# A graph network on one core: VectorE's early operations reordered and thinned, filler matmuls on TensorE, later epilogues

## The reference

```python
msg = concat([x[dst], x[src], edge_attr]) @ W + b      # per edge
h   = relu(segment_sum(msg, dst))                      # per node
```

## Time and profile before

| | us |
|---|---|
| median of 3 runs | 204.44 (204.09 to 204.75) |
| the profiled execution's own time | 204.8 |
| its span, first to last instruction | 202.9 |
| TensorE matmul busy | 172.5 (85%) |
| VectorE busy | 170.4 (84%) |
| ScalarE busy | 119.3 (59%) |
| GpSimd busy | 34.0 (17%) |
| chain of waits, by engine | PE 61%, DVE 31%, issue 3%, DMA 2%, ACT 2% |

### The profile page before, as it was taken

The page is one execution under the profiler, slowest core; times in us unless marked ns, Lnnn a source line. Parts: engine busy times, 40 slices in busy tenths (PEclk is TensorE's granted clock), DMA queues, the critical chain, the costliest instruction groups (busy, mean ns, idle before and its releaser), DMA issues.

```text
span 202.9 us, 5018 instructions
## 1 busy us (share of the span) xinstructions
PE 172.5 (85%) x2019; PEld 163.2 (80%) x2019; DVE 170.4 (84%) x420; ACT 119.3 (59%) x234; POOL 34.0 (17%) x58
## 2 busy tenths in 40 slices
PE   0414389799999999999999999999996999999950
PEld 0103379788999999989899999899996999999940
DVE  0898999999999999999999979921039999999874
ACT  2236657678899999998898999984310201121101
POOL 8478832000400240006006000000000000000000
PEclk9999999999999999999999999999999999999995
DMA  1334210000000000000000000000000010011010
GB/s 42 105 84 126 59 14 3 0 3 3 3 0 4 0 0 3 3 2 3 0 1 3 3 0 3 2 3 0 3 0 0 5 38 3 7 36 25 22 24 19
DMA packets 8959, 3.34 MB, mean 16 GB/s; under 512 B 8168, under 2 KB 8485, under 8 KB 8935
## 3 DMA queue, kind: packets, MB, share of 16 engines
q1 hardware_dynamic: 8135, 2.07, 4.9%
q0 software_dynamic: 800, 0.93, 1.8%
HBM read 2.18 MB, written 0.81 MB: 15 GB/s over the span
## 4 chain that ended last, share of the span: by engine, by line
PE 61%; DVE 31%; issue 3%; DMA 2%; ACT 2%; DVEq 0%; ACTq 0%
PE acc L989 17%; PE pset L1035 17%; DVE oh L517 15%; PE pset L975 12%; PE acc L1035 7%; PE epb L1018 2%; PE epb L1029 2%; DMA adj<-in_dst 2%; DVE adj L508 2%; PE epb L1006 2%; DVE adj L470 1%; DVE u L546 1%; DVE x L531 1%; ACT u L843 1%; DVE adj L456 1%
## 5 line engine op out<-in xcount | busy, mean ns | idle before, releaser
L517 DVE TENSOR_TENSOR oh<-iota,keys 128x2000 bf16<-128x2000 bf16 (+1 forms) x79 | 90.9, 1179 | 1.0 <-ACT keys L811 0.5
L828 ACT ACTIVATE adj<-pset 125x1000 bf16<-125x1000 f32 (+7 forms) x100 | 81.4, 840 | 13.8 <-PE pset L975 11.9
L989 PE MATMUL acc<-x,adj 125*125 125x195 bf16 x625 | 67.9, 252 | 0.0
L975 PE MATMUL pset<-oh 128*125 128x125 bf16 x625 | 53.8, 230 | 9.0 <-DVE oh L517 8.9
L989 PEld LDWEIGHTS acc<-x,adj 125*125 125x125 bf16 x625 | 57.3, 139 | 0.3
L975 PEld LDWEIGHTS pset<-oh 128*125 128x125 bf16 x625 | 47.8, 146 | 11.9 <-ACT adj L828 4.9
L1035 PE MATMUL pset<-z,adj 125*125 125x192 bf16 x425 | 36.8, 246 | 1.8 <-DVE x L673 1.8
L1035 PEld LDWEIGHTS pset<-z,adj 125*125 125x125 bf16 x425 | 35.5, 136 | 2.0 <-DVE x L673 2.0
L917 ACT ACTIVATE x<-x 125x192 f32<-125x192 f32 (+2 forms) x6 | 2.6, 428 | 34.5 <-DVE x L682 34.5
L1035 PE MATMUL acc<-z,adj 125*125 125x192 bf16 x200 | 17.5, 246 | 0.0
L1035 PEld LDWEIGHTS acc<-z,adj 125*125 125x125 bf16 x200 | 16.8, 136 | 0.0
(11 more groups left out here) (123 smaller groups left out, 159.9 us busy)
## 6 DMA issues: line engine op xcount, KB each, us to landing
x_nat<-in_x_tiles SPq DMA_DIRECT2D x1, 406.2 KB
x_nat<-in_x_tiles SPq DMA_DIRECT2D x1, 375.0 KB
out<-x SPq DMA_DIRECT2D x2, 187.5 KB
out<-x SPq DMA_DIRECT2D x3, 93.8 KB
adj<-in_dst SPq DMA_DIRECT2D x1, 208.5 KB
out<-x SPq DMA_DIRECT2D x1, 125.0 KB
adj<-in_edges,adj POOLq DMA_INDIRECT x5, 4.6
adj<-in_edge_attr,adj POOLq DMA_INDIRECT x5, 3.4
```

The source lines that it names most:

```text
L517: dve.tensor_tensor(out=oh[k % 3][:, 0:n, :, :], in0=iota2[:, 0:Q, :].unsqueeze(1).broadcast_to([128, n, Q, 2]), in1=keys[:, k * SET:k * S ...
L828: ins = act.activation(adj4[0:Q, g, :, i * WD:(i + n) * WD].rearrange("p h (w e) -> p h w e", e=WD), rows[:, w - k * SET:w - k * SET + n, ...
L975: ins = pe.matmul(pset[k % 2][0:Q, i // 4, i % 4 * 128:i % 4 * 128 + WD * G], oh[k % 3][:, i, :, 0], oh[k % 3][:, i, :, 1], start=True, st ...
L989: ins = pe.matmul(acc[g % 2][0:Q, 0:XW], adj4[0:Q, g, h, :], x3[:, h, :], start=(h == 0), stop=(h == G - 1))
```

## The change

- L446 goes from VectorE to ACT, and `offset` uses an operation with one input in place of two; `ones` is gone. Part 4's offset is put behind the first keys.
- `rest_of_x`, `low_of_x` and `bias_rest` of the first part stand ahead of the first one-hot; `rest_of_x(1)`, `low_of_x(1)` and `bias_rest(1)` stand behind sets 3, 5 and 7.
- The distances of parts 1 to 4 are ACT's (`distances`, five blocks ahead of the key block).
- The mask operations on VectorE are gone; SP issues nine small SBUF-to-SBUF DMAs that lay the bias rows in `bw`, once ACT has cast the third part.
- `KEY_BLOCK` and `SUM_SET` are later; part 0's attribute sums go one by one behind sets 10 to 14. Epilogues 0 and 1 turn at blocks 18 and 25 (13 and 22 before); the others keep their block. ACT does `scale_x` one block earlier.
- Layer 1 begins when the first part of x is split; it waits for the second at group 12. In block 0, set 4 is built behind layer 1's matmuls.
- TensorE gets filler matmuls of 512 columns on a zeroed piece of `adj`: 10 at the very start, 9 between the picks and the first key transposes, 4 behind these, 1 behind each of the sets 1 to 3.
- `base_of` for groups 0 to 15 stands ahead of the last two `z_rest`/`z_low`; the rest behind batch 0. The last step of a batch is two operations over all its groups in place of one per group.

```diff
-KEY_BLOCK = {1: 5, 2: 20, 3: 38, 4: 48}
-SUM_SET = {1: 12, 2: 25, 3: 41, 4: 51}
+KEY_BLOCK = {1: 7, 2: 22, 3: 38, 4: 48}
+SUM_SET = {0: 10, 1: 17, 2: 29, 3: 45, 4: 54}
+TURN = (18, 25, 32, 41, 50, 60, 69, 78, 82)
...
+        still = adj[:, 4 * G * Q:4 * G * Q + 512]
...
+            dve.memset(still, 0.0).then_inc(still_ready, 1)
             dve.wait_ge(dst_in, 16)
-            dve.tensor_scalar(rows16[:, 0:EC], dst_rows[:, 2:EC + 2], -float(MID), None, ALU.add).then_inc(rowsf_ready, 1)
...
-                link(dve.scalar_tensor_tensor(out=junk[:, j, :], in0=row[:, 0:EC], scalar=thr_mid[:, j:j + 1],
-                                              in1=ones[:, :], op0=ALU.is_lt, op1=ALU.mult,
-                                              accum_out=cnt2[:, j:j + 1]))
+                link(dve.tensor_scalar(junk[:, j, :], row[:, 0:EC], thr_mid[:, j:j + 1], None, ALU.is_lt, ALU.add,
+                                       accum_out=cnt2[:, j:j + 1]))
...
-            for j in range(1, J):
+            for j in range(1, 4):
                 offset(j)
...
+            rest_of_x(0, 0, XA)
             key_distances(0)
             key_tiles(0)
             key_sums(0)
-            rest_of_x(0, 0, XA)
+            low_of_x(0, 0, XA)
+            offset(4)
+            bias_rest(0)
             dve.wait_ge(consts, 7)
             dve.wait_ge(keys_ready, 1)
             onehots(0)
             onehots(1)
-            bias_rest(0)
-            low_of_x(0, 0, XA)
             onehots(2)
+            onehots(3)
             rest_of_x(1, XA, G)
-            bias_rest(1)
-            attr_sums(0, 0, WD)
-            onehots(3)
-            low_of_x(1, XA, G)
-
-            for k in range(4, NSETS):
+            onehots(4)
+
+            for k in range(5, NSETS):
...
-                if k == 10:
...
+                if k == 5:
+                    low_of_x(1, XA, G)
+                if k == 7:
+                    bias_rest(1)
                 for j in range(1, J):
                     if k == KEY_BLOCK[j] + 2:
-                        key_distances(j)
+                        dve.wait_ge(dist_ready, j)
+                        key_tiles(j)
                     if k == KEY_BLOCK[j] + 3:
-                        key_tiles(j)
-                    if k == KEY_BLOCK[j] + 4:
                         key_sums(j)
...
+            base_of(0, BATCHES[1][1])
+            base_of(BATCHES[1][1], BATCHES[2][1])
             z_rest(last - 1)
...
-                for k in range(n):
-                    ins = dve.tensor_scalar(f_v[i % 2][:, k, :], f_p[:, k, 0:C], f_c[:, k:k + 1], f_r[:, k:k + 1],
-                                            ALU.subtract, ALU.mult)
-                flink(ins)
+                flink(dve.tensor_tensor(o, p, c.unsqueeze(2).broadcast_to([Q, n, C]), ALU.subtract))
...
+                flink(dve.tensor_tensor(vv, o, r.unsqueeze(2).broadcast_to([Q, n, C]), ALU.mult))
...
+            act.wait_ge(dst_in, 16)
+            act.activation(rows16[:, 0:EC], dst_rows[:, 2:EC + 2], ACT.Copy, bias=-float(MID)).then_inc(rowsf_ready, 1)
...
-            for j in range(1, J):
-                copy_row(j)
+            copy_row(1)
+            copy_row(2)
             cast_x(0, 0, XA)
+            for j in range(3, J):
+                copy_row(j)
+            cast_bias(0)
+            cast_middle_x(0, 0, XA)
             copy_keys(acc[0][:, 0:2 * Q], 0)
-            cast_middle_x(0, 0, XA)
+            cast_bias(1)
+            def distances(j):
+                act.wait_ge(pairs_in[j], 16)
+                act.activation(d_f[:, j, :], pairs[:, j, 1::2], ACT.Identity, bias=thr_neg[:, j:j + 1])
+                act.activation(q_f[:, j, :], pairs[:, j, 0::2], ACT.Copy, scale=1.0 / Q, bias=-float(Q // 2) / Q)\
+                   .then_inc(dist_ready, 1)
...
+                if w <= 6 * G < end:
+                    act.wait_ge(bw_in, 16 * 3 * EP)
...
-                    if b == turn_block(i) - 1:
+                    if b == turn_block(i) - 2:
                         scale_x(i)
...
+            def keep_going(n):
+                for _ in range(n):
+                    pe.matmul(epb[:, 1, :], still[:, 0:128], still, start=True, stop=True)
+            keep_going(10)
...
+            keep_going(9)
             turn_keys(acc[0], 0)
+            keep_going(4)
...
                     if g == 0:
-                        pe.wait_ge(xl_ready, 2)
+                        pe.wait_ge(xm_ready, 1)
+                        pe.wait_ge(xl_ready, 1)
...
+            sp.wait_ge(bp_ready, 3)
+            for m in range(EP):
+                for part in range(3):
+                    mine = slice(VFROM + m * KB + part, VFROM + (m + 1) * KB, 3)
+                    sp.dma_start(bw[mine, m, :], bpart[mine, part, :]).then_inc(bw_in, 16)
```

More of the change, by code:

```diff
@@ L627, in _ @@
             z_low(last - 2)
-            reduce_sums(G - 1)
-            z_rest(last - 1)
-            z_low(last - 1)
-            z_rest(last)
-            z_low(last)
-            dve.tensor_reduce(deg_sum[:, :], stats[:, :, 0], AX.X, ALU.add).then_inc(deg_ready, 1)
             fc = [0]
@@ L662, in _ @@
                 dve.wait_ge(se_in[j], 16)
-            dve.wait_ge(rest_ready, len(EPILOGUES))
             base_of(0, BATCHES[1][1])
+            base_of(BATCHES[1][1], BATCHES[2][1])
+            z_rest(last - 1)
+            z_low(last - 1)
+            z_rest(last)
+            z_low(last)
+            dve.tensor_reduce(deg_sum[:, :], stats[:, :, 0], AX.X, ALU.add).then_inc(deg_ready, 1)
             na = 0
@@ L716, in _ @@
                 if i == 0:
-                    base_of(BATCHES[1][1], G)
+                    base_of(BATCHES[2][1], G)
                 if i == 1:
@@ L793, in copy_row, with cast_bias @@
                 act.activation(row16[:, j, :], row[:, 0:EC + 1], ACT.Copy).then_inc(rows_copied, 1)
-            for j in range(1, J):
-                copy_row(j)
+            copy_row(1)
+            copy_row(2)
+            def cast_bias(k):
+                if k == 0:
+                    act.wait_ge(b_in, 16 * 2 * EP)
+                else:
+                    act.wait_ge(br_ready, k)
+                act.activation(bpart[VHALF:128, k, :], brows[VHALF:128, :] if k == 0 else brest[VHALF:128, k - 1, :], ACT.Copy).then_inc(bp_ready, 1)
             def cast_x(i, a, b):
@@ L868, in cast_middle @@
                 act.activation(z3[:, a:b, C:2 * C], u[i % 2][:, 0:b - a, 0:C], ACT.Copy).then_inc(mid_ready, 1)
-            def cast_bias(k):
-                if k == 0:
-                    act.wait_ge(b_in, 16 * 2 * EP)
-                else:
-                    act.wait_ge(br_ready, k)
-                act.activation(bpart[VHALF:128, k, :], brows[VHALF:128, :] if k == 0 else brest[VHALF:128, k - 1, :], ACT.Copy).then_inc(bp_ready, 1)
-            cast_bias(0)
             evacuate(0)
-            cast_bias(1)
             cast_x(1, XA, G)
-            evacuate(1)
-            cast_bias(2)
+            for k in range(1, LEAD):
+                evacuate(k)
             cast_middle_x(1, XA, G)
-            for k in range(2, LEAD):
-                evacuate(k)
             for b in range(NSETS):
@@ L888, in _ @@
                     evacuate(b + LEAD)
+                if b == 3:
+                    cast_bias(2)
+                for j in range(1, J):
+                    if b == KEY_BLOCK[j] - 5:
+                        distances(j)
                 for j in range(1, J):
@@ L988, in layer1 @@
                 for h in range(h0, h1):
+                    if g == 0 and h == XA:
+                        pe.wait_ge(xm_ready, 2)
+                        pe.wait_ge(xl_ready, 2)
                     ins = pe.matmul(acc[g % 2][0:Q, 0:XW], adj4[0:Q, g, h, :], x3[:, h, :],
@@ L1050, in _ @@
                     i += n
+                if b == 0:
+                    build(LEAD)
                 for j in range(1, J):
```

54 lines of the change are left out of this document (21 added, 33 removed).

## The result

The changed kernel takes 198.86 us (median of 6 runs, 198.11 to 199.45); the kernel before, run beside it, 204.41 (204.09 to 204.92). The ratio is 0.9724, with a 95% interval of 0.970 to 0.9748. Run again later it took 198.55, ratio 0.9713 (0.9697 to 0.973). The forecast was 198.6, with a range of 196.2 to 201.8. The profiled execution took 199.06, its span is 197.2.

What follows compares the result with a forecast made beforehand. VectorE was taken to bound building up to 46 us, TensorE afterwards. Gains of 3.7 (to layer 1's end), 2.0 and 0.1 sum to 5.8 off 204.8, giving 199.0, or 198.6 for the median; range 196.2 to 201.8.

Steps and rivals of the forecast that it cites:

- The start: Up to the first one-hot: gains and costs nearly cancel, one-hot 0 at 15.9 (15.99 before), bounds 15.0 and 16.8.
- VectorE's work up to set 16: First one-hot to set 16: 5.0 us leaves VectorE, 0.3 lost to waits; set 16 at 40.9, gain 4.8.
- Sets 17 to 21, the give-back: Sets 17 to 21: attribute sums load VectorE and epilogue 0 is still to be paid; 1.4 us lost, bounds 0.8 and 1.8.
- Set 22 to the end of layer 1: TensorE bounds here, only its gaps may go: 0.3 us gained, bounds 1.8 gained and 1.0 lost.
- The change to layer 2: After layer 1: base_of for 16 groups fills VectorE's idle 5.57, TensorE's 2.00 wait goes; gain 2.0, bounds 1.7 and 2.0.
- The last batch: Last batch: L711's three operations become two of 0.36; gain 0.1, bounds -0.1 and 0.3.
- The nine bias DMAs: On SP: nine issues of 0.3 us and a landing of some 3 end at 34; price nothing, cover 8 us.
- The offset's new form: VectorE's offsets: no change taken; by the skill each of four SBUF offsets might lose about 0.22 us, up to 0.7 lower.
- this rival: ACT becomes the bound: 0.5 to 1 us in each of three places; with ACT or a late start, 201.5, chance 0.20.
- The other sign: Building up to set 16: the forecast is wrong if set 16 comes later than 42.5.
- the key transposes that I had named: Set 27's key transposes, part 2 in block 22: no idle of TensorE expected, with a cover of 0.3 us.
- eight layer-1 matmuls in 0.69 in the first block: Layer 1's first block: a sign of the forecast, eight matmuls already taking 0.69 us, the higher clock level.

Runs made afterwards that it cites:

- run three: The changed kernel with ACT's copies of picked rows 3 and 4 ahead of its cast of x: 198.03 us, ratio 0.9702.
- run four: The changed kernel with the distances of parts 1 to 4 on VectorE again in place of ACT: 199.70 us, ratio 0.9764.
- five: The changed kernel with the bias rows laid by VectorE's masks behind set 10 again, without the nine DMAs: 201.54 us, ratio 0.9858.
- nine: The changed kernel with copied rows first, early turns, scale_x one block ahead, and part 0's attribute-sum round trip ahead of the bias DMAs: 196.55 us, ratio 0.9626.
- run ten: The changed kernel with copied rows first, early turns and part 0's attribute-sum round trip ahead of the bias DMAs, scale_x two blocks ahead: 195.84 us, ratio 0.9588.
- run seven: The changed kernel with ACT's scale_x one block ahead of the turn in place of two: 199.34 us, ratio 0.9742.
- six: The changed kernel with epilogues 0 and 1 at blocks 13 and 22, second key block at 20, part 0's sums behind sets 4 to 8: 198.38 us, ratio 0.9696.
- eight: The changed kernel with rows 3 and 4 copied before the x cast, early turns, key block and sums, and scale_x one block ahead: 198.15 us, ratio 0.9685.
- run two: The changed kernel without any of the 26 filler matmuls: 198.99 us, ratio 0.9733.

## Why the prediction was right, step by step

- **The start.** The pick chain is 0.94 earlier, as forecast (1.0), and ACT's 0.56 is near the 0.53 of the row it was taken from. The first fillers ended at 5.65 and the first pick stands at 5.80 with and without them, so they cost nothing. The open point was when x lands; it landed at 10.09, near the late end, and with the copies of rows 3 and 4 behind the cast the gain was gone. I put one-hot 0 at 15.9, inside bounds of 15.0 and 16.8, and it came at 16.61. This term was off by 0.7, and run three gave 0.7 to 0.8 back by moving one line. What was wrong is the weight: "if at 10 or 11 there is no gain" was in the text, and the value taken was nearer to the other end.
- **VectorE's work up to set 16.** Forecast 5.0 off and 0.3 lost, measured 4.62. Runs four and five put two terms back singly: the distances cost 0.46 (0.45), the masks 2.3 in all (2.16). The bound that the windows named is shown.
- **Sets 17 to 21, the give-back.** This term failed in size. Forecast was a loss of 1.4, with bounds of 0.8 and 1.8. The stretch took 6.72, and with epilogue 0's 2.0 still to be paid that is 0.6 more than the 8.12 before: outside the bounds. VectorE needed 6.7 us for the five sets in place of 7.5; one group sum fell into them and not two, and TensorE waited 0.23 once.
- **Set 22 to the end of layer 1.** Forecast 0.3 gained, measured 0.1 (2.69 - 0.80 = 1.89 lost, of which epilogue 0's 2.0 are not this term's). The sum hides two larger parts. Up to set 35 some 0.7 was lost, in the crowd where epilogues 0 and 1 and the key block stand close together; with the other 0.6 that is the 1.3 which runs nine and ten win back by moving the turns (together with the second key block and part 0's sums). From 35 on 0.80 was gained, where I had said that TensorE's own work is the bound. Run four gives 0.76 of it to the distances, 0.48 at one place; `scale_x` has only 0.14 there by run seven, its other 0.39 lie between 16 and 35.
- **The change to layer 2.** 1.97 of 2.0, and 1.8 to 2.0 in time by itself. The cover of `z_rest` held with 0.20 us left.
- **The last batch.** 0.11 for 0.1. The subtraction over three groups runs in the gap behind the first small operation:

```profile
193.22 0.16 DVE L687 TENSOR_TENSOR x<-x 125x3 f32<-125x3 f32 x1
193.30 0.35 DVE L689 TENSOR_TENSOR x<-x 125x192 f32<-125x192 f32 x1
...
194.07 0.36 DVE L694 TENSOR_TENSOR x<-x 125x192 f32<-125x192 f32 x1
```

- **The nine bias DMAs.** Forecast nine issues of 0.3 us and a cover of 8. They took 5.65, 0.63 each, twice as long, and ended at 36.48 in place of 34. The cover was there in the changed kernel, with part 0's sums at set 14 (SP issues them at 39.05); the price shows as soon as those sums come earlier (runs six and eight).
- **The offset's new form.** L472 takes 0.65 us as L470 did. The estimate from the Trainium skill (VectorE: DVE Perf Modes, "What auto-detection actually checks") of 0.22 less each is not what this counting operation did; the measurement decides.
- **The rivals.** ACT did become the brake in places. I had written that I am wrong if TensorE's waits for ACT's evacuations add up to over 1.5 us, and the page of the changed kernel has 1.9 (idle time before the group, and what ended it); in the kernel before there is none:

```profile
L1003 PE MATMUL acc<-x,adj 125*125 125x195 bf16 x625 | 66.5, 249 | 1.9 <-ACT adj L835 1.9
```

These are three waits. The first, 0.75 at 24.21, lies where VectorE is the bound; the other two, 0.53 at 61.65 and 0.66 at 98.46, are 1.2 us on TensorE's own path. So this rival held in part, at 1.2 of the 1.5 to 3 us that it named, and the forecast's sum had no term for it. Run seven takes both waits away and is slower, so moving `scale_x` doesn't give them back.

The other sign, set 16 later than 42.5, did not come (41.66). TensorE is not idle at the key transposes that I had named, and layer 1's last matmul starts at 135.08. The sign "eight layer-1 matmuls in 0.69 in the first block" came from the chain of waits, which counts to the start of what follows; the timeline gives 0.85 for the same work at the higher level, and the first block took 0.91 and the second 0.86. So it was met but for 0.06. The lower clock level in layer 1's first block cost nothing in run two; at the first builds it costs 0.4, as the section on the hardware shows.

The number is better than its parts. In the forecast's own terms the errors are +0.7 at the start, +0.1 up to set 16, -0.8 in sets 17 to 21 and +0.2 behind them. They cancel, and that they do is luck: the mechanism (what bounds which stretch, and the 2.0 us of `base_of`) held, and the placing of the losses did not.

## What to carry to other kernels

Follow one full engine's list of work between two named pieces, and price what leaves it; outside that stretch the same microseconds are worth nothing, or all, depending on which engine is level there (run four: 0.46, nothing, nothing, 0.48). When small work is moved to a queue that looks idle, count what will stand behind it: nine tiny DMAs cost nothing until the first turn wanted the sums behind them 5 us earlier (45.84 against 51.16 us). A pure wait of a full engine, as TensorE's 2.00 us for `base_of`, is the safest gain: it came whole, alone and in company.

## What the runs showed of the hardware

The fillers raised TensorE's clock and did not hold it. That they raised it shows in the last pick's matmul at 9.10: 0.39 us with fillers, 0.62 without (run two). The page of the changed kernel has the granted clock in 40 slices of 4.9 us:

```profile
PEclk9966699999999999999999999999999999999996
```

The third to fifth slice, about 10 to 25 us, read 0.6. Within them it fell, rose and fell again: the windows give 0.50 from 10 to 12 us, 0.89 from 15 to 17 and 0.50 from 17 to 22. The first fall, to the level of 1.2 GHz, came while TensorE was at the beginning of nine fillers in a row; from 6 to 8 us it had been busy for 0.66 of 2 us. The Trainium skill (TensorE: Matmul & The Clock Gate, "What's actually happening") has activity release the throttle and idleness bring it back; the trace agrees in both directions, but with the fall coming late, on top of new work. In the kernel before the same row reads 9 in these slices although the builds of sets 0 and 1 took the same 2.23 us; there the durations, not the row, tell the level.

When the second fall comes differs from one execution to the next, and it is worth 0.4 us. The window from 17 to 20 us (the column before the last two is the granted clock), the builds and VectorE's wait for ACT's cast of x, first in the changed kernel's first trace, then in its rerun's:

```profile
17.00:20.00 3.00, 2.14 (x17) 1.88 (x17) 3.00 (x4) 0.98 (x1) 2.39 (x3) 0.50 0.50 135
...
17.86 2.23 PE L985 MATMUL pset<-oh 128*125 128x125 bf16 x16 [1.95 <-DVE oh L518]
...
24.98 1.03 DVE L532 TENSOR_TENSOR x<-adj,x 125x832 bf16<-125x832 f32 x1 [0.69 <-ACT x L795]
```

```profile
17.00:20.00 3.00, 1.81 (x17) 1.32 (x17) 3.00 (x4) 1.48 (x2) 2.39 (x3) 0.86 0.48 126
...
17.77 0.69 PE L985 MATMUL pset<-oh 128*125 128x125 bf16 x8 [1.96 <-DVE oh L518]
...
24.47 1.03 DVE L532 TENSOR_TENSOR x<-adj,x 125x832 bf16<-125x832 f32 x1 [0.27 <-ACT x L795]
```

At the higher level the builds end sooner, ACT evacuates them sooner and comes sooner to its cast, and VectorE, which is the bound there, waits 0.42 less. Set 3 is built 3.64 us after set 0 in place of 4.07, and the 0.42 stays up to the end of the span (196.7 against 197.2; the other 0.1 is there at set 0). The eleven traces of the changed kernel and its variants fall into the same two groups: 3.64 or 3.65 us in the five in which the higher level lasted beyond 18 us (the rerun, three, eight, nine, ten), 4.06 or 4.07 in the six in which it had ended by 17 or never come (the first trace, two, four, five, six, seven). The link over ACT is read from these rows and from ACT's order (`cast_middle_x` stands behind the evacuation of set 3); no run changes the clock alone, and why the level ends sooner in one execution than in another of the same program, none tells.

SP needed 0.63 us for each of nine DMAs between SBUF addresses (4 rows three partitions apart, 1 KB) in the changed kernel, and 0.77 in run ten (6.89 for nine), against 0.27 to 0.29 for its issues of the bias rows from DRAM in the changed kernel's trace.
